# One Trainium2 core, fp32 graph layers: every fourth weight piece fetched as 64, 32 and four times eight partitions, the others as 64, 32 and 32

## What is computed

```python
h = relu(layernorm(x))
q, k, v = h @ wq.T + bq, h @ wk.T + bk, h @ wv.T + bv
q2, k2, v2 = q @ wiq.T + biq, k @ wik.T + bik, v @ wiv.T + biv     # 16 heads of 64
attn = softmax(q2 @ k2.T / 8 + mask)                               # mask from the edges and their types
x = x + (attn @ v2) @ wo.T + bo
h = relu(layernorm(x))
u = h @ root + bias + sum(mean_of_messages(r) @ weight[r] for r in range(8))
z = concatenate([u, h]) @ w_gate + b_gate
out = x + tanh(u) * z + h * (1 - z)
```

## Time and profile before

| | |
|---|---|
| median of three runs | 228.41 us (227.95 to 232.79) |
| the profiled execution | 227.98 us, span of its instructions 225.8 us |
| PE matmul busy | 216.0 us, 96% of the span |
| DVE, ACT, POOL busy | 80.6, 22.3, 23.2 us |
| granted TensorE clock | 1.0 in the whole span |
| read from HBM | 75.97 MB |

### The profile page before, as it was taken

The page is one execution under the profiler, slowest core; times in us unless marked ns, Lnnn a source line. Parts: engine busy times, 40 slices in busy tenths (PEclk is TensorE's granted clock), DMA queues, the critical chain, the costliest instruction groups (busy, mean ns, idle before and its releaser), DMA issues.

```text
span 225.8 us, 10194 instructions
## 1 busy us (share of the span) xinstructions
PE 216.0 (96%) x4797; PEld 210.1 (93%) x4797; DVE 80.6 (36%) x138; ACT 22.3 (10%) x41; POOL 23.2 (10%) x53
## 2 busy tenths in 40 slices
PE   2999998998999999999999999999999999999994
PEld 2889988998999999898999999999999999999993
DVE  2479638050399930555738500000000000000624
ACT  2550000000020110132033000000000000000101
POOL 2271005500000000010000940000000000000000
PEclk9999999999999999999999999999999999999999
DMA  6999999999999999999999799999999999998002
GB/s 225 366 393 422 421 422 421 380 376 385 363 386 385 328 383 376 363 359 399 412 360 379 209 306 398 328 383 388 398 380 361 369 350 338 356 363 332 6 3 70
DMA packets 14684, 77.01 MB, mean 341 GB/s; under 512 B 4874, under 2 KB 5138, under 8 KB 5428
## 3 DMA queue, kind: packets, MB, share of 16 engines
q1 hardware_dynamic: 14112, 75.96, 88.5%
q10 hardware_dynamic: 532, 0.42, 0.6%
HBM read 75.97 MB, written 0.39 MB: 338 GB/s over the span
## 4 chain that ended last, share of the span: by engine, by line
PE 95%; DMA 2%; issue 1%; DVE 1%; ACT 0%
PE acc L780 81%; PE acc L1027 4%; DMA x_sb<-in_x 2%; PE turn L968 1%; PE side L828 1%; PE side L968 1%; PE side L1027 1%; PE turn L856 1%; DVE stats L505 1%; PE acc L798 1%; PE turn L798 0%; PE turn L872 0%; PE side L839 0%; PE turn L839 0%; PE acc L872 0%
## 5 line engine op out<-in xcount | busy, mean ns | idle before, releaser
L780 PE MATMUL acc<-mean,raw 128*64 128x96 f32 x2048 | 84.7, 246 | 0.0
L780 PEld LDWEIGHTS acc<-mean,raw 128*64 128x64 f32 x2048 | 84.6, 137 | 0.0
L780 PE MATMUL acc<-hT,raw 128*64 128x96 f32 x1024 | 44.4, 247 | 0.3 <-issue 0.3
L780 PEld LDWEIGHTS acc<-hT,raw 128*64 128x64 f32 x1024 | 42.9, 137 | 1.4 <-issue 1.1
L743 DVE TENSOR_TENSOR uT<-acc,uT 128x384 f32<-128x384 f32 x2 | 1.1, 558 | 80.9 <-PE acc L780 80.9
L780 PE MATMUL acc<-kT,raw 128*64 128x96 f32 x512 | 22.1, 246 | 0.8 <-issue 0.8
L780 PEld LDWEIGHTS acc<-kT,raw 128*64 128x64 f32 x512 | 21.5, 137 | 1.3 <-issue 1.2
L780 PE MATMUL acc<-qT,raw 128*64 128x96 f32 x512 | 22.0, 246 | 0.7 <-issue 0.7
L780 PEld LDWEIGHTS acc<-qT,raw 128*64 128x64 f32 x512 | 21.4, 137 | 1.0 <-issue 1.0
L780 PE MATMUL acc<-uT,raw 128*64 128x96 f32 x256 | 12.6, 266 | 0.0
L780 PEld LDWEIGHTS acc<-uT,raw 128*64 128x64 f32 x256 | 12.2, 152 | 0.3 <-ACT uT L409 0.2
(11 more groups left out here) (177 smaller groups left out, 148.3 us busy)
## 6 DMA issues: line engine op xcount, KB each, us to landing
raw<-in_weights SPq DMA_DIRECT2D x284, 256.0 KB, 4.7
raw<-in_weights SPq DMA_DIRECT2D x1, 1024.0 KB, 5.9
x_sb<-in_x SPq DMA_DIRECT2D x1, 192.0 KB, 3.5
x_sb<-in_x ACTq DMA_DIRECT2D x1, 192.0 KB, 3.7
out<-out_rows SPq DMA_DIRECT2D x1, 192.0 KB, 2.1
out<-out_rows ACTq DMA_DIRECT2D x1, 144.0 KB, 2.4
out<-out_rows SPq DMA_DIRECT2D x1, 48.0 KB, 2.2
bias_rows<-in_biases ACTq DMA_DIRECT2D x1, 36.0 KB
```

The lines of the kernel that those rows point to most:

```text
L780: mm = pe.matmul(a[g * HD:(g + 1) * HD, b, c * N:(c + 1) * N], raw[:, s, at:at + HD], moving(k0 + k), start=opens and k0 == 0 and c == 0 a ...
```

## The change

`transfers(n)` gives other lists of partitions. Each piece but the first is now a transfer of the 64 even partitions, one of the 32 partitions 1, 5, 9 and so on, and the remaining 32 partitions (3, 7, 11 and so on) either as one transfer or, where n % 4 is 3, as four transfers of eight partitions, one for each block of 32 partitions. `landed(n)` is worked out from the same lists, so PE's waits follow. The bytes, the buffers and the order of the pieces stay as they are.

```diff
 def transfers(n):
 
     if n == 0:
         return [slice(0, P)]
-    return [slice(j, P, 4) for j in range(4)]
+    if n % 4 == 3:
+        return [slice(0, P, 2), slice(1, P, 4), *(slice(32 * i + 3, 32 * i + 32, 4) for i in range(4))]
+    return [slice(0, P, 2), slice(1, P, 4), slice(3, P, 4)]
```

## The result

The changed kernel takes 244.27 us (243.96 to 247.79) against 228.18 us: 1.0709 times the time before, 95% interval 1.0674 to 1.0744. The ratio is that of the faster executions, without the two slow ones of 247.79 us and 232.79 us. Its profiled execution has a span of 241.8 us where the span before was 225.8, so 16.0 us have to be found in the trace.

What follows compares the result with a forecast made beforehand. PE's own work was taken as the bound, with the weight stream ahead. The profiled 227.98 us + 0 + 0 + 0 gave 228.0 us, set at 228.2 us to fit the runs; range 225.5 to 232.5 us.

Steps and rivals of the forecast that it cites:

- What bounds the kernel, and what the gaps are: PE's own work bounds; its three "issue" gaps, 1.8 us by the matmuls, are instruction blocks arriving late.
- Part 1: SP's weight issues: 285 transfers become 268; the 17 saved, 10.7 us of SP, are worth 0 us.
- Part 2: DMA engines: eight-row transfers use eight engines, 34 rows against 30 over four pieces; cost on the path 0 us.
- Late pieces: Weight pieces reaching PE: the 2.2 us cover holds against at most 1.24 us by piece 7, so 0 us.
- Part 3: PE's instruction blocks behind weight rows: from -1.8 us (-3.4 by weight loads) to +12.5 us, taken as 0 us.
- Half the blocks gain and half lose: Instruction blocks: those on lighter engines come sooner, those on heavier ones do not, a sum of 0 us.
- both upper bounds: Instruction-block gaps if the early loss per block held for the other 29: +6.7 us by matmuls, +12.5 by weight loads.
- A block of margin of 5.3 us: PE's instruction supply: PE has 128 pairs in hand, 5.3 us, before a late block stops it.
- rival C: Slower: blocks over the heavier eight engines repeatedly late, past PE's 5.3 us in hand; 231.3 to 234.2 us, chance 0.27.
- B: PE's gaps close as lighter engines deliver the blocks: 226.2 us, by the weight loads 224.6; chance 0.20.
- D: Heavy pieces reach PE late because loaded engines fall behind: worst case 11 us, 239 us; chance 0.03.
- the 34 pieces: Sign in PE's last long stretch of matmuls: still about 90 us from 121 us on.

Runs made afterwards that it cites:

- the moved gaps: Changed kernel with 40 small unused transposes at the start of TensorE's program: 243.41 us in one execution.
- the wide matmuls: Each pair of 64-column weight loads and matmuls made one of 128 columns: 291.50 us on the changed kernel, 291.25 us on the kernel before.
- The 64, 32 and 32 version: Changed kernel without eight-row transfers, every piece but the first in 64, 32 and 32 partitions: 237.51 us, 1.0404 times the kernel before.
- the 71 idle issues: The 64, 32 and 32 version plus one small unused load issued for each piece but the first: 234.94 us, 1.0303 times the kernel before.
- sixteens: Changed kernel with the four eight-partition transfers of every fourth piece made two of 16 partitions: 249.01 us, 1.0899 times the kernel before.

## Why the prediction was wrong

**What bounds the kernel, and what the gaps are:** right. No piece came late in the changed kernel, and the reading of the gaps as ends of instruction blocks, argued from the distances, was shown by the packets of q8, by the moved gaps and by the wide matmuls.

**Part 1, "17 issues saved are worth 0 us":** the first step that failed. SP's issue time isn't on PE's path, but it held the stream back: at 2.55 us a piece it handed out rows about as fast as the engines took them (2.48 us), and with issues saved the queues fill. The 64, 32 and 32 version, with 214 issues, lost 4.0%; two transfers to a piece, with 143, lost 7.0%; with SP held to five pieces ahead of PE the changed kernel lost 5.0 and not 7.1%. How much of it is the pace alone isn't shown: the transfers differ in shape as well, and the 2.5 us of the 71 idle issues lie within the noise. I had the numbers (9.4 us against 10.5 for four pieces) and used them for late pieces alone.

**Part 2, the work by engine:** the count of eight engines was right, the weight that I gave it wasn't shown. With 16 rows to each transfer and all engines even, the loss was greater. What the small transfers do goes, as far as is shown, by how their partitions are divided: 249.0 us for sixteens, 237.6 us for the same pieces split by columns. Whether the eights hurt only in that way or also by their 34 to 30 was not tried by itself and stays open. Late pieces: 0 us, as forecast.

**Part 3, the sum of 0 for the blocks:** the term that was mis-sized, and the one that decided. "Half the blocks gain and half lose" has no support: no group of blocks came sooner. The measured cost passed both upper bounds. By the matmuls 1.8 us had given +6.7 at most, and their gaps grew by 11.4 us (13.2 - 1.8); by the weight loads 3.4 us had given +12.5, and theirs grew by 14.0 (17.4 - 3.4). The bounds took the early loss for each block as a ceiling, and it rose as well: the longest gap went from 0.8 to 1.9 us. On top of that each stopped run of 128 takes 5.50 us for 5.29; the piece matmuls of the chain grew by 3.9 us, which the bound by the matmuls left out. "A block of margin of 5.3 us" was also too much: 1.0 us to move the packet and 1.4 us behind it come off, so that a wait of about 3 us is enough for a gap. The range ended at 232.5 because I cut rival C in half and tied it to the loaded engines.

**The rivals:** C is what happened, in its mechanism (blocks later than the 5.3 us that PE has in hand, gaps 128 apart, behind 60 us too) and not in its place: it was priced for half of the blocks, 231.3 to 234.2 us, it hit in stretches of the whole kernel, and the loaded engines that it named as the reason aren't needed for it. B and D did not occur. That the time before was steady at a point just short of this (three gaps among eight blocks in the early stretch) spoke for C and I read it as half a defence.

**The signs:** 268 issues, 13264 packets, no wait for `raw`, SP's longer wait and "issue" over 5 us, 127 or 128 matmuls apart, all came as the text said for C. One sign failed: the 34 pieces that should still take about 90 us took 96.2 (from 130.63 to 226.78 us), 4.3 us of them gaps.

## What to carry to other kernels

When an engine runs a long unrolled program at full rate, the weight stream shares its DMA engines with that program's instructions; look for "issue" gaps at a constant distance in instructions, and see how full the queues are once the data is ahead. Holding the queues short gave the changed kernel 2% back and gained nothing for the kernel before, where late pieces took the place of the gaps. An issuing engine that is "only just quick enough" may be the throttle that keeps it so: before transfers are merged to save issues, ask who else needs those queues. And choose the partitions of a transfer with care, since neighbouring ones halved the rate here; a count of bytes and rows doesn't show that.

## What the runs showed of the hardware

32 neighbouring partitions in each transfer gave about 227 GB/s, 32 with a step of 4 gave 421. TensorE went on 1.3 to 1.5 us after a packet of 16 KB of its instructions had landed, in all 17 gaps of the changed kernel; the next packet started 1.1 us later with the weight stream over, 2.8 to 4.8 us later within it, and 5.8 to 6.4 us later in the stream of 227 GB/s. Four transfers of 64 partitions with rows of 4 KB cost 1 to 3% against four of 32 with rows of 8 KB. An issue on SP took about 0.6 us for 8 to 64 partitions: its median was 0.60 us in the changed kernel, and 16 in a row, of 256 KB and of 64 KB, took 10.59 us. For 128 partitions with rows of 4 KB the median was 0.43 us and the longest 3.15. Two fp32 matmuls with 64 weight columns each, 96 columns moved, take 82.7 ns together and one with 128 columns takes 111.6.
